# Another order of tasks for ScalarE, SyncE and TensorE in a one-core Mamba and routed-expert kernel

## The chip, the core and the metric

The kernel runs on one core of a Trainium2 chip. The core has TensorE (matrix products, PE in the profile), VectorE (DVE), ScalarE (ACT), GpSimd (POOL) and SyncE (SP, which issues nearly all DMAs). Each engine runs its own instructions strictly in order and waits on semaphores that the others raise. The metric is the device time of one execution in microseconds (us); lower is better. The kernel before takes 2237.96 us, the median of three runs (2236.62 to 2238.84).

## The reference, cut to what matters

```python
x = x + tanh(g_xattn) * mamba(ctx, z=layernorm(x))      # x: [4, 1024, 1024], ctx: [4, 1024, 512]
x = x + tanh(g_ffn)   * experts(layernorm(x))

def mamba(h, z):                                        # 1024 channels, 16 states each
    u  = silu(causal_conv4(in_proj_w @ h) + conv_b)
    dt_low, B, C = split(x_proj_w @ u)                  # 32, 16 and 16 rows
    dt = softplus(dt_proj_w @ dt_low + dt_proj_b)
    state[t] = state[t-1] * exp(dt[t] * A) + dt[t] * u[t] * B[t]
    y[t] = sum over the 16 states of state[t] * C[t] + D * u[t]
    return y * silu(z)

def experts(x):                                         # 16 experts that share one 1024x1024 weight
    S = softmax(x @ router_w + router_b)
    G, idx = top 256 of the 4096 tokens for each expert
    return scatter_add(G * (x[idx] @ expert_w + expert_b))
```

Since all experts share one weight, the product x @ expert_w is computed once for every token, and what each token receives is that row, with the bias, times the sum of its chosen scores. All of it is in float32.

## The kernel before

**Tiling.** The 4 x 1024 tokens are cut into eight halves of 512 tokens (h = 0 to 7), and the 1024 channels into eight blocks of 128 (e = 0 to 7). For each half there are 8 x 16 = 128 rows of states, and each row is one scan over 512 tokens on VectorE (`scan_of`, L1002). A half has 64 *slots*, and a slot is two scans. All five engines run a loop over the slots of a half, and in each slot they do the tasks whose place in a table is that slot; a number below 0 or over 63 means the half before or after. Everything but the scans is software-pipelined by these tables: while half h is scanned, the front of half h + 1 (input projection, convolution, `silu_u`, `xproj`, `low`) and the back of half h − 1 (norm, router logits, expert product) are done in between.

**What a scan needs.** A decay exp(dt·A), computed by ScalarE into one of three PSUM banks (`decays`, L794, one for each scan, so that ScalarE can be at most three scans ahead of VectorE), and an input dt·u·B in one of eight state buffers, made by VectorE (`times_b`, L989) for five groups of eight and by GpSimd (L1236) for the other three. After the scan GpSimd multiplies by C (`times_c`, L1248), and TensorE turns the product and adds it up in the bank pY (`sum_states`, L586), which frees the state buffers. At the end of a channel block VectorE multiplies pY by the gate (`y_out`, L1010) and adds it to x (`add_x`, L1018).

**ScalarE's other tasks.** Some are short copies out of PSUM: `gate_out` (L806, turned gate, after TensorE's `turn_gate`, L597), `xfT_out` (L847), `logits_out` (L876), `unit_out` (L861, a finished 128x512 piece of the expert product), `low` (L760, after TensorE's `xproj`, L563), `xin_ready` (L746, after `inproj`, L554). Three kinds are what is called a burst below: `softplus` (L767, eight times in a half), `silu_u` (L754, once in a half, 4096 columns) and `gate_silu` (L868, twice in a half, 4 x 512 columns). A burst needs another function table, so a table load stands before it and another one (L936) behind it. In a slot the order on ScalarE is: decays, diagonal, `xin_ready`, `low`, `dtu_copy`, the bursts, and then `late`, which holds `gate_out`, `xfT_out`, `logits_out`, `norm_x2`, the row sums and `unit_out`.

**TensorE** does in a slot first `inproj`, `xproj` and `dtproj` (L572, the input of `softplus`), and then `late`: `sum_states`, `turn_gate`, `logits`, `turn_xf` (L612), and `product_step` (L647). A unit of the product (128 tokens x 512 columns) is eight steps, each with its own 128x512 piece of expert_w that SyncE loads into a ring of NRING places (`load_step`, L395). The bank pA is shared by `inproj`, `xproj` and `turn_gate`, the bank pD by `dtproj`, `turn_xf` and `logits`. `turn_xf` waits until the logits before it have been copied out by ScalarE. For the last half (h = 7) the expert weight is resident in the memory that B's rows held, and the ring isn't used.

**SyncE** also walks the slots, and blocks at each DMA that must wait. A load of dt_proj's weights (`load_dtp`, L353) waits for the `dtproj` two blocks before it; a load into the ring waits for the step that last read the place; `load_gate` (L362) waits for the last `turn_gate` that read its tile.

**The end.** After the scans of half 7 come the rest of the product of half 6 and 7, the softmax, a search for each expert's threshold in 30 steps, and a stage in which all rows come back from memory, are scaled, added and written out.

Of the kernel before, what the change touches and what calls it, by code (L numbers as in the profile page):

```python
# [13 lines left out]
P = 128  # L14
# [31 lines left out]
IN_SLOT = [-77, -73] + [GQ * j - 85 for j in range(2, E)]  # L46
# [3 lines left out]
HALO_SLOT, SILU_SLOT = [-24], [-20]  # L50
XP_SLOT, LOW_SLOT = [-18, -18, -17, -17], [-14]
# [14 lines left out]
SZT_SLOT = [GQ * e + 9 for e in range(5)] + [43, 50, 65]  # L66
# [6 lines left out]
XF_SLOT = [s + 4 for s in LN2_SLOT]  # L73
# [7 lines left out]

UNIT_SLOT = [104 + 8 * i for i in range(2 * TT)]
STEP_SLOT = [s + min(k, E - 2) for s in UNIT_SLOT for k in range(E)]
UO_SLOT = [s + 8 for s in UNIT_SLOT]

SLOTTED = 2
NRING, NPIECE = 4, 3
# [4 lines left out]
def at(slots, g, h):  # L92

    return [(i, h - s // G) for i, s in enumerate(slots) if s % G == g and 0 <= h - s // G < NC]
# [29 lines left out]
def mamba_moe(nc, x, ctxT, g_xattn, g_ffn, winT, conv_w, conv_b, xpT, dtpT, dt_b, a_log, dvec,  # L124
              router_w, router_b, expert_w, expert_b, consts, row_masks, out):
    with ExitStack() as ctx:
        def sb(name, shape, dt=F32):
            return ctx.enter_context(nc.sbuf_tensor(name, shape, dt))
# [30 lines left out]
        mhalf = sb("mhalf", [P, B, E])  # L159
# [22 lines left out]
        mv1 = szT[0][:, 160:160 + 2 * NC * TT].rearrange("p (b e s) -> p b e s", b=B, e=E)  # L182
        coef = szT[1][:, 0:TT * NC].rearrange("p (t c) -> p t c", t=TT)
# [149 lines left out]
        def _(sp):  # L333
# [94 lines left out]
            WK_SLOT = [s - 2 for s in STEP_SLOT]  # L428
# [3 lines left out]
            DTW_SLOT = [DTP_SLOT[e] - 17 for e in range(E)]  # L432
# [65 lines left out]
            load_dtp(0, 3)  # L498
# [240 lines left out]
        def _(act):  # L739
# [174 lines left out]
            def half(h):  # L914
                for g in range(G):
# [8 lines left out]
                    for e, k in at(DCP_SLOT, g, h):  # L924
                        dtu_copy(k, e)
                    steps_due = at(SP_SLOT, g, h)
# [10 lines left out]
                    late(h, g)  # L937
# [33 lines left out]
        def _(dve):  # L971
# [138 lines left out]
            nc.vector.memset(mhalf[:], -0.5).then_inc(s_c, 1)  # L1110
# [111 lines left out]
        def _(pool):  # L1222
# [40 lines left out]
            def rstd2(h, t):  # L1263
                wait(pool, s_bn, n(h, 3 * TT, 3 * t + 3))
                nc.gpsimd.tensor_tensor(rs2[:, t:t + 1], ve2[:, t:t + 1], mhalf[:, 0, 0:1], ALU.pow).then_inc(s_pr, 1)
                pool.wait_ge(s_pr, n(h, TT, t + 1))
                nc.gpsimd.tensor_tensor(nb2[:, t:t + 1], nm2[:, t:t + 1], rs2[:, t:t + 1], ALU.mult).then_inc(s_rs2, 1)
# [22 lines left out]
            def ln1_rstd(rows, k):  # L1290
                pool.wait_ge(s_ln1v, k)
                nc.gpsimd.tensor_tensor(ln1[:, rows, 0, :], ve1[:, rows, :], mhalf[:, rows, :], ALU.pow).then_inc(s_rs1, 1)
# [63 lines left out]
```

## Time and profile before

| what | value |
|---|---|
| median of three runs | 2237.96 us |
| the profiled execution, its time and its span | 2250.82 us, 2249.0 us |
| DVE busy | 1936.2 us (86%) |
| POOL busy | 1711.8 us (76%) |
| PE busy | 1668.7 us (74%) |
| ACT busy | 1371.7 us (61%) |
| DVE busy between 980 and 1220 us | 218.31 of 240 us |
| POOL busy between 980 and 1220 us | 213.52 of 240 us |
| mean granted TensorE clock | 0.880 |
| last scan ends | at about 1972.7 us |

How to read it: the busy shares are averages over the whole span, and the stages differ. From about 66 to 1973 us the scans run, about 240 us to a half; from there to about 2090 us VectorE mostly waits, and then the search and the last stage follow. A row of the timeline gives the start, the length, engine, line, operation, tiles, shapes and count, and in brackets how long the engine was idle before it and what ended that idle time. "SPq" is SyncE's queue.

### The profile page before, as it was taken

The page shows a single profiled execution, that of the slowest core. Times are in us where ns is not written, and L with a number is a line of the kernel's source. Part 1 is how long each engine was busy: PE and PEld are TensorE (multiplying, and loading weights), DVE is VectorE, ACT ScalarE, POOL GpSimd, SP SyncE. Part 2 cuts the span into 40 slices and gives each one's busy share as a digit, 9 for nine tenths or more (in the row PEclk, how much of TensorE's full clock was granted, in tenths as well). Part 3 has the DMA queues.
Part 4 walks back from the last instruction along what each step waited for, and adds up shares of the span by engine and source line. Part 5 has one row for each costly group of instructions (what it writes and reads, how often), then busy time and mean ns, then how long its engine had stood idle before and what let it go on. Part 6 is the DMA issues. An engine that isn't in the chain of part 4 may idle for free.

```text
span 2249.0 us, 23467 instructions
## 1 busy us (share of the span) xinstructions
PE 1668.7 (74%) x7564; PEld 1064.5 (47%) x7564; DVE 1936.2 (86%) x2081; ACT 1371.7 (61%) x2326; POOL 1711.8 (76%) x606
## 2 busy tenths in 40 slices
PE   7467676678887888778887888787878787788720
PEld 2235445445554555445554555454555565544310
DVE  7989999988999899988997999889997899910587
ACT  3545766675778676766787676757786767622000
POOL 0578999987899899988998899878998999920000
PEclk9677788889898999999998999899998899999865
DMA  9500141134735383527443563337343734376078
GB/s 370 220 15 29 63 174 66 38 108 147 265 111 169 99 301 113 179 67 279 139 160 96 192 226 119 126 126 270 118 150 100 277 109 136 99 239 231 0 300 353
DMA packets 144219, 358.69 MB, mean 159 GB/s; under 512 B 15586, under 2 KB 18146, under 8 KB 134882
## 3 DMA queue, kind: packets, MB, share of 16 engines
q1 hardware_dynamic: 140354, 343.57, 43.1%
q10 hardware_dynamic: 3744, 13.63, 1.5%
q8 instruction: 61, 1.00, 0.2%
q14 instruction: 60, 0.49, 0.1%
HBM read 310.48 MB, written 46.66 MB: 159 GB/s over the span
## 4 chain that ended last, share of the span: by engine, by line
DVE 25%; PE 23%; issue 16%; POOL 13%; ACT 11%; DMA 9%; SPq 1%; ACTq 1%; DVEq 0%; POOLq 0%
DVE states L1002 15%; POOL states L1248 8%; PE pM L647 7%; PE pY L586 5%; PE pA L554 4%; POOL states L1236 4%; DMA sz<-in_x 4%; DMA wk<-in_expert_w 3%; DVE states L989 3%; ACT pDec L794 3%; DVE u L979 2%; PE pA L563 2%; ACT L936 2%; ACT sz L868 2%; DMA bbc<-x_scratch 1%
## 5 line engine op out<-in xcount | busy, mean ns | idle before, releaser
L1248 POOL TENSOR_TENSOR states<-states,cbc 128x2048 f32<-128x2048 f32 x256 | 1158.3, 4532 | 114.2 <-ACT carry L778 83.0
L794 ACT ACTIVATE pDec<-steps,an 128x512 f32<-128x512 f32 x1024 | 691.7, 687 | 441.9 <-DVE states L1002 439.6
L586 PE MATMUL pY<-con,states 128*128 128x128 f32 x4096 | 578.6, 303 | 144.3 <-POOL states L1248 144.1
L1002 DVE TENSOR_TENSOR_SCAN states<-pDec,carry,states 128x512 f32<-128x512 f32 x512 | 625.2, 1265 | 57.2 <-ACT pDec L794 57.0
L586 PEld LDWEIGHTS pY<-con,states 128*128 128x128 f32 x4096 | 532.9, 158 | 272.0 <-POOL states L1248 220.6
L1002 DVE TENSOR_TENSOR_SCAN states<-pDec,states 128x512 f32<-128x512 f32 x512 | 594.7, 1205 | 66.2 <-ACT pDec L794 65.7
L647 PE MATMUL pM<-wk,xfT 128*128 128x512 f32 x896 | 473.0, 634 | 78.7 <-DMA wk<-in_expert_w 75.4
L1236 POOL TENSOR_TENSOR states<-dtu,bbc 128x1024 f32<-128x1024 f32 x192 | 454.2, 2366 | 98.9 <-PE pY L586 81.4
L989 DVE TENSOR_TENSOR states<-pU,bbc 128x1024 f32<-128x1024 f32 x320 | 385.3, 1204 | 17.3 <-PE pY L586 14.0
L554 PE MATMUL pA<-ctx_sb,win 128*128 128x512 f32 x448 | 233.8, 671 | 53.3 <-issue 32.5
L647 PEld LDWEIGHTS pM<-wk,xfT 128*128 128x128 f32 x896 | 154.3, 202 | 173.3 <-issue 96.3
L554 PEld LDWEIGHTS pA<-ctx_sb,win 128*128 128x128 f32 x448 | 94.2, 217 | 180.5 <-issue 148.1
L582 PE MATMUL pY<-ddiag,u 128*128 128x128 f32 x512 | 84.5, 317 | 106.1 <-issue 88.7
L582 PEld LDWEIGHTS pY<-ddiag,u 128*128 128x128 f32 x512 | 77.5, 225 | 148.9 <-issue 129.2
L979 DVE SCALAR_TENSOR_TENSOR u<-pA,cw,u 128x509 f32<-128x509 f32 x171 | 125.1, 732 | 2.1
L936 ACT ACT_TABLE_LOAD x86 | 110.3, 1283 | 1.5
L1227 POOL TENSOR_TENSOR dtu<-steps,u 128x512 f32<-128x512 f32 x64 | 81.4, 1272 | 11.8 <-ACT steps L767 11.8
L1062 DVE TENSOR_REDUCE mx<-lg 128x4 f32<-128x64 f32 x8 | 1.7, 208 | 96.2 <-ACT lg L876 96.2
L767 ACT ACT_TABLE_LOAD x64 | 82.1, 1283 | 1.1
L572 PE MATMUL pD<-xpr,dtp 32*128 32x512 f32 x128 | 75.5, 670 | 5.1 <-ACT xfT L847 3.3
L861 ACT COPY stg<-pM 128x512 f32<-128x512 f32 x56 | 32.4, 579 | 73.2 <-PE pM L647 73.2
L612 PE MATMUL pD<-con,xr 128*128 128x128 f32 x240 | 39.9, 293 | 38.0 <-ACT lg L876 38.0
(174 smaller groups left out, 1394.9 us busy)
## 6 DMA issues: line engine op xcount, KB each, us to landing
wk<-in_expert_w SPq DMA_DIRECT2D x448, 256.0 KB, 4.2
bbc<-bc_scratch SPq DMA_DIRECT2D x32, 1024.0 KB, 6.5
cbc<-bc_scratch SPq DMA_DIRECT2D x32, 1024.0 KB, 9.0
sz<-in_x SPq DMA_DIRECT2D x16, 1024.0 KB, 7.4
xt<-in_x SPq DMA_DIRECT2D x15, 1024.0 KB, 5.6
win<-in_winT SPq DMA_DIRECT2D x58, 256.0 KB, 2.7
x_scratch<-xt SPq DMA_DIRECT2D x14, 1024.0 KB, 6.9
xr<-x_scratch SPq DMA_DIRECT2D x28, 512.0 KB, 4.2
```

The costliest lines, as they stand in the source:

```text
L554: mm = pe.matmul(pA[:], win[j % 2][:, part, :], ctx_sb[:, part, :], start=(part == 0), stop=(part == KC - 1))
L582: mm = pe.matmul(pY[:, eT(t)], u[h % 2][:, e, eT(t)], ddiag[:], start=(t == 0), stop=False)
L586: mm = pe.matmul(pY[:, eT(t)], states[g % NST][:, i, eT(t)], ident, start=False, stop=(q == QG - 1 and i == QN - 1 and t == TT - 1), is_tr ...
L647: pe.matmul(bank[:], piece_of(h, 2 * t + k // 4)[:, k % 4, :], weights, start=(k == 0), stop=(k == E - 1)) \
L767: nc.scalar.activation(dt[e % 2], pD[:], ACT.Softplus, bias=dtb[:, e:e + 1]).then_inc(s_sp, 1)
L794: nc.scalar.activation(pDec[bank_of(h, k)][:], dt[e % 2], ACT.Exp, scale=an[:, k:k + 1]).then_inc(s_dec, 1)
L936: nc.scalar.preload_act_table_set(EXP)
L979: nc.vector.scalar_tensor_tensor(out=dst, in0=bank[:, 0:T - HALO + i], scalar=cw[:, j, i:i + 1], in1=dst, op0=ALU.mult, op1=ALU.add).then_ ...
L989: nc.vector.tensor_tensor(states[g % NST], spread(pU), bbc[:, QN * q:QN * (q + 1), :], ALU.mult) \
L1002: nc.vector.tensor_tensor_scan(st, pDec[bank_of(h, k)][:], st, 0.0 if h % HB == 0 else carry[:, e, k % NS:k % NS + 1], ALU.mult, ALU.add). ...
L1236: nc.gpsimd.tensor_tensor(states[g % NST], spread(dtu[e % 2]), bbc[:, QN * q:QN * (q + 1), :], ALU.mult) \
L1248: nc.gpsimd.tensor_tensor(st, st, cbc[:, QW * q:QW * (q + 1), :], ALU.mult).then_inc(s_hc, 1)
```

## The change

Only the places of tasks change, with the ring of expert weights and the room for it; no arithmetic does.

```diff
-IN_SLOT = [-77, -73] + [GQ * j - 85 for j in range(2, E)]
+IN_SLOT = [-79, -74] + [GQ * j - 85 for j in range(2, E)]
-HALO_SLOT, SILU_SLOT = [-24], [-20]
-XP_SLOT, LOW_SLOT = [-18, -18, -17, -17], [-14]
+HALO_SLOT, SILU_SLOT = [-24], [-22]
+XP_SLOT, LOW_SLOT = [-20, -20, -19, -19], [-16]
-SZT_SLOT = [GQ * e + 9 for e in range(5)] + [43, 50, 65]
+SZT_SLOT = [GQ * e + 9 for e in range(5)] + [43, 48, 65]
-XF_SLOT = [s + 4 for s in LN2_SLOT]
+XF_SLOT = [s + 5 for s in LN2_SLOT]
-STEP_SLOT = [s + min(k, E - 2) for s in UNIT_SLOT for k in range(E)]
-UO_SLOT = [s + 8 for s in UNIT_SLOT]
+STEP_SLOT = [s + k for s in UNIT_SLOT for k in (0, 1, 1, 2, 3, 3, 4, 5)]
+UO_SLOT = [s + 7 for s in UNIT_SLOT]
-NRING, NPIECE = 4, 3
+NRING, NPIECE = 5, 3
...
-            WK_SLOT = [s - 2 for s in STEP_SLOT]
+            WK_SLOT = [s - 3 for s in STEP_SLOT]
-            DTW_SLOT = [DTP_SLOT[e] - 17 for e in range(E)]
+            DTW_SLOT = [DTP_SLOT[e] - 15 for e in range(E)]
...
             load_dtp(0, 2)
-            load_dtp(0, 3)
...
                     for e, k in at(DCP_SLOT, g, h):
                         dtu_copy(k, e)
+                    late(h, g)
                     steps_due = at(SP_SLOT, g, h)
...
                     if steps_due or silus or gates:
                         nc.scalar.preload_act_table_set(EXP)
-                    late(h, g)
```

Modulo 64, the places near the end of a half are now: `silu_u` in slot 42 (44 before), the four parts of `xproj` in 44 and 45 (46 and 47), `low` in 48 (50), the seventh gate turned in 48 (50) and copied in 49 (51), the first two input projections of the half after next in 49 and 54 (51 and 55). A unit's steps stand in six slots (seven before, of which the last held two), and its copy in the seventh slot after its first step (the eighth before). The fifth place of the ring takes 2 KB of each partition; for it the constant −0.5 shrinks to one column, and the copy that the first norm needs moves into a tile that is free then (one more short memset).

**ScalarE, where `silu_u` stands** (middle of the scans of half 4; `u1` is the front of half 5, `szT0` a gate's copy, `lg` the logits). Before:

```order
L794 ACTIVATE pDec0<-steps,an 128x512
L778 COPY carry<-states1 128x2
L794 ACTIVATE pDec1<-steps,an 128x512
L754 ACT_TABLE_LOAD
L754 ACTIVATE u1<-u1 128x4096
L936 ACT_TABLE_LOAD
L806 COPY szT0<-pA 128x512
L876 COPY lg<-pD 128x16
L794 ACTIVATE pDec2<-steps,an 128x512
```

With the change:

```order
L795 ACTIVATE pDec0<-steps,an 128x512
L807 COPY szT1<-pA 128x512
L755 ACT_TABLE_LOAD
L755 ACTIVATE u1<-u1 128x4096
L938 ACT_TABLE_LOAD
L795 ACTIVATE pDec1<-steps,an 128x512
L779 COPY carry<-states0 128x2
L795 ACTIVATE pDec2<-steps,an 128x512
L795 ACTIVATE pDec0<-steps,an 128x512
L779 COPY carry<-states1 128x2
L795 ACTIVATE pDec1<-steps,an 128x512
L807 COPY szT0<-pA 128x512
```

The burst stands four decays earlier, the short copy `szT1` of its slot in front of it, and the copies `szT0` and `lg`, which stood right behind it, now come four decays after it.

**ScalarE, from the product's copy to the next burst** (the same half, slots 47 to 50; `stg` is `unit_out`, `xpr` is `low`). Before:

```order
L861 COPY stg<-pM 128x512
L794 ACTIVATE pDec1<-steps,an 128x512
L778 COPY carry<-states3 128x2
L794 ACTIVATE pDec2<-steps,an 128x512
L798 ACTIVATE ddiag<-con,dvt 128x128
L767 ACT_TABLE_LOAD
L767 ACTIVATE steps<-pD,dtb 128x512
L936 ACT_TABLE_LOAD
L794 ACTIVATE pDec0<-steps,an 128x512
L778 COPY carry<-states0 128x2
L794 ACTIVATE pDec1<-steps,an 128x512
L760 ACTIVATE xpr<-pA,csc 64x512
```

With the change:

```order
L862 COPY stg<-pM 128x512
L795 ACTIVATE pDec2<-steps,an 128x512
L779 COPY carry<-states3 128x2
L795 ACTIVATE pDec0<-steps,an 128x512
L761 ACTIVATE xpr<-pA,csc 64x512
L795 ACTIVATE pDec1<-steps,an 128x512
L779 COPY carry<-states3 128x2
L795 ACTIVATE pDec2<-steps,an 128x512
L799 ACTIVATE ddiag<-con,dvt 128x128
L807 COPY szT1<-pA 128x512
L768 ACT_TABLE_LOAD
L768 ACTIVATE steps<-pD,dtb 128x512
```

Between the product's copy and the burst there are four decays in place of two, and both `xpr` and the seventh gate's copy `szT1` (which came later than this piece before) stand in front of the burst.

**TensorE, where the second input projection stands** (the same half, slots 52 to 56; `win1` is its weight, `dtp0` that of `dtproj`). Before:

```order
L582 MATMUL pY<-ddiag,u0 128x128 x4
L586 MATMUL pY<-con,states0 128x128 x16
L647 MATMUL pM<-wk,xfT 128x512 x2
L586 MATMUL pY<-con,states1 128x128 x16
L647 MATMUL pM<-wk,xfT 128x512 x2
L554 MATMUL pA<-ctx_sb,win1 128x512 x4
L572 MATMUL pD<-xpr,dtp0 128x512
L586 MATMUL pY<-con,states2 128x128 x16
```

With the change:

```order
L583 MATMUL pY<-ddiag,u0 128x128 x4
L587 MATMUL pY<-con,states0 128x128 x16
L648 MATMUL pM<-wk,xfT 128x512 x2
L555 MATMUL pA<-ctx_sb,win1 128x512 x4
L587 MATMUL pY<-con,states1 128x128 x16
L573 MATMUL pD<-xpr,dtp0 128x512
L587 MATMUL pY<-con,states2 128x128 x16
```

The projection stands one group of sums earlier, and no longer right in front of `dtproj`. The convolution of the block before it, for which it waits, also stands two slots earlier on VectorE (52 and 53 in place of 54 and 55).

## Rows read from the trace of the kernel before

**Rows 1.** Who waited for whom, whole span: total us, times, longest us

```profile
DVE states L1002 <- ACT pDec L794: 122.7, 71, 4.9
...
ACT stg L861 <- PE pM L647: 73.2, 20, 6.6
...
ACT sz L868 <- DMA sz<-in_x: 10.9, 7, 3.1
```

**Rows 2.** SyncE's own waits, whole span

```profile
SPq L353 <- PE pD L572: 739.8, 60, 31.1
```

**Rows 3.** Timeline of ScalarE in half 4, slots 44 to 58

```profile
1197.56 1.28 ACT L754 ACT_TABLE_LOAD   x1
1198.85 3.62 ACT L754 ACTIVATE u<-u 128x4096 f32<-128x4096 f32 x1
...
1204.33 0.71 ACT L794 ACTIVATE pDec<-steps,an 128x512 f32<-128x512 f32 x1
...
1219.92 0.58 ACT L861 COPY stg<-pM 128x512 f32<-128x512 f32 x1 [6.64 <-PE pM L647]
...
1234.40 0.59 ACT L806 COPY szT<-pA 128x512 f32<-128x512 f32 x1 [3.29 <-PE pA L597]
...
1258.75 0.69 ACT L767 ACTIVATE steps<-pD,dtb 128x512 f32<-128x512 f32 x1 [4.27 <-PE pD L572]
```

**Rows 4.** Timeline of VectorE, the same stretch

```profile
1197.85 0.67 DVE L1010 TENSOR_TENSOR pY<-pY,szT 128x512 f32<-128x512 f32 x1
1198.43 1.21 DVE L989 TENSOR_TENSOR states<-pU,bbc 128x1024 f32<-128x1024 f32 x1
...
1205.14 4.57 DVE L1002 TENSOR_TENSOR_SCAN states<-pDec,states 128x512 f32<-128x512 f32 x4 [1.53 <-ACT pDec L794]
...
1261.54 2.34 DVE L1002 TENSOR_TENSOR_SCAN states<-pDec,states 128x512 f32<-128x512 f32 x2 [3.82 <-ACT pDec L794]
```

**Rows 5.** Timeline of TensorE, the same stretch

```profile
1204.69 1.08 PE L612 MATMUL pD<-con,xr 128*128 128x128 f32 x4 [5.88 <-ACT lg L876]
...
1210.81 1.88 PE L647 MATMUL pM<-wk,xfT 128*128 128x512 f32 x4
1212.62 3.65 PE L563 MATMUL pA<-u,xp 128*64 128x512 f32 x8
1216.20 1.97 PE L586 MATMUL pY<-con,states 128*128 128x128 f32 x16
...
1251.10 6.56 PE L554 MATMUL pA<-ctx_sb,win 128*128 128x512 f32 x8 [3.24 <-issue]
```

**Rows 6.** VectorE's waits between 482.2 and 524.0 us (half 1, slots 44 to 52)

```profile
DVE states L1002 <- ACT pDec L794: 8.4, 5, 2.6
DVE states L989 <- PE pY L586: 1.9, 2, 1.3
DVE pY L1010 <- PE pY L586: 1.2, 1, 1.2
```

**Rows 7.** VectorE's waits between 1683.2 and 1723.2 us (half 6, the same slots)

```profile
DVE states L1002 <- ACT pDec L794: 8.3, 5, 2.7
DVE states L989 <- PE pY L586: 2.6, 2, 1.5
```

**Rows 8.** VectorE's waits between 538.0 and 547.8 us (half 1, slot 58)

```profile
DVE states L1002 <- ACT pDec L794: 3.4, 1, 3.4
```

**Rows 9.** VectorE's waits between 1497.0 and 1506.9 us (half 5, slot 58)

```profile
DVE states L1002 <- ACT pDec L794: 3.5, 1, 3.5
```

**Rows 10.** Who waited for whom between 1975 and 2042 us

```profile
PE pM L647 <- DMA wk<-in_expert_w: 9.9, 6, 3.8
```

**Rows 11.** Timeline of ScalarE, copies of finished units behind the last scan

```profile
1991.59 0.58 ACT L861 COPY stg<-pM 128x512 f32<-128x512 f32 x1 [2.15 <-PE pM L647]
...
2039.47 0.58 ACT L861 COPY stg<-pM 128x512 f32<-128x512 f32 x1 [6.37 <-PE pM L647]
...
2077.07 0.58 ACT L861 COPY wk<-pM 128x512 f32<-128x512 f32 x1 [2.29 <-PE pM L647]
```

More of the change, by code:

```diff
@@ L158, in mamba_moe @@
         ddiag = sb("ddiag", [P, P])
-        mhalf = sb("mhalf", [P, B, E])
+        mhalf = sb("mhalf", [P, 1])
         ctx_sb = sb("ctx_sb", [P, KC, T])
@@ L182, in mamba_moe @@
         mv1 = szT[0][:, 160:160 + 2 * NC * TT].rearrange("p (b e s) -> p b e s", b=B, e=E)
+        mhalves = szT[0][:, 280:280 + NC * TT].rearrange("p (b e) -> p b e", b=B)
         coef = szT[1][:, 0:TT * NC].rearrange("p (t c) -> p t c", t=TT)
@@ L1109, in _ @@
             nc.vector.memset(one[:], 1.0)
-            nc.vector.memset(mhalf[:], -0.5).then_inc(s_c, 1)
+            nc.vector.memset(mhalf[:], -0.5)
+            nc.vector.memset(mhalves, -0.5).then_inc(s_c, 1)
             dve.wait_ge(s_w, 16 * NW)
@@ L1264, in rstd2 @@
                 wait(pool, s_bn, n(h, 3 * TT, 3 * t + 3))
-                nc.gpsimd.tensor_tensor(rs2[:, t:t + 1], ve2[:, t:t + 1], mhalf[:, 0, 0:1], ALU.pow).then_inc(s_pr, 1)
+                nc.gpsimd.tensor_tensor(rs2[:, t:t + 1], ve2[:, t:t + 1], mhalf[:], ALU.pow).then_inc(s_pr, 1)
                 pool.wait_ge(s_pr, n(h, TT, t + 1))
@@ L1291, in ln1_rstd @@
                 pool.wait_ge(s_ln1v, k)
-                nc.gpsimd.tensor_tensor(ln1[:, rows, 0, :], ve1[:, rows, :], mhalf[:, rows, :], ALU.pow).then_inc(s_rs1, 1)
+                nc.gpsimd.tensor_tensor(ln1[:, rows, 0, :], ve1[:, rows, :], mhalves[:, rows, :], ALU.pow).then_inc(s_rs1, 1)
             ln1_rstd(slice(0, 1), 1)
```

## The prediction

> **What bounds the kernel now.** I read the busy shares first, then who waited for whom, then the timelines of three engines side by side around VectorE's longest waits, and last the stretch behind the last scan. While the scans run, VectorE is busy 218.31 of 240 us, so about 20 us of each half are not VectorE's own work (table of the profile, 980 to 1220 us). The list of waits says what those are: 122.7 us in 71 waits of a scan for its decay [rows 1]. ScalarE is busy 61% of the span, so it isn't short of time: it is late at a few places, because it is held by a burst or by somebody else's result. These places are the same in each half:
>
> - Slots 44 to 52. In half 4 `silu_u` with its two table loads holds ScalarE from 1197.56 to 1203.8 [rows 3]; the first scan behind it waits 1.53 us [rows 4]. The logits' copy stands behind the burst, and TensorE waits 5.88 us for it [rows 5]. From there TensorE works without a gap for 15.2 us, up to the unit's end, for which ScalarE's copy waits 6.64 us with no decay ready behind it; and the seventh gate's copy waits 3.29 us more [rows 3]. VectorE loses 11.5 us here in half 1 (8.4 + 1.9 + 1.2) [rows 6] and 10.9 us in half 6 [rows 7]; the six halves 1 to 6 lie between 8.8 and 12.0 (half 4) and make 63.6 us, 10.6 each. Half 0, which has no product beside it, loses 1.7.
> - Slot 58. TensorE waits 3.24 us for a convolution, makes the second input projection in 6.56 us [rows 5] and only then `dtproj`; `softplus` waits 4.27 us for it [rows 3] and VectorE 3.82 [rows 4]. It is 3.4 us in half 1 [rows 8] and 3.5 in half 5 [rows 9], 15.3 in the five halves 1 to 5, and 1.3 in half 0. Half 6, which has no such projection to make (there is no half 8), has no wait there: that is the control for the cause.
> - Slots 6 and 38, behind `gate_silu`. The one in slot 6 is longer, since the gate's tile lands late: ScalarE waits 10.9 us for it in 7 cases [rows 1].
>
> Behind the last scan TensorE is the bound. The units of half 6, whose weights come through the ring, end 12.0 us apart (2039.47 − 1991.59 over 4); the next four, with resident weights, 9.4 us (2077.07 − 2039.47 over 4) [rows 11]. 9.9 us are plain waits for the ring [rows 10].
>
> **The change, part by part.**
>
> *`silu_u` two slots up.* The burst is 1.28 + 3.62 + 1.28 = 6.2 us, then comes a decay of 0.7. Before, VectorE had beside it the gate's product (0.67 [rows 4]), the add behind it (as long), two inputs (1.21 each) and two scans (1.14 each from the 4.57 of four), 6.0 us in all, and 1.5 were left open. In slot 42 the product and the add (they belong to slots 43 and 44) and one input fall behind the burst: 2.3 us of scans, one input of 1.2 and some 0.3 of a scan already running are the cover, 3.8 us, and the chain is 0.6 (the gate copy now in front) + 6.2 + 0.8 = 7.6. The hole grows from 1.5 to about 3.8, so 2.3 to 2.4 us are lost in each of seven halves. The halo sums on GpSimd for `silu_u` end some 2 us behind its new start in the odd halves' fronts, while the table loads; that costs nothing to 1 us, and I take nothing.
>
> The trace shows 6.2 us for this burst, from the table load at 1197.56 to the copy after the second load, so a load costs 1.28 and nothing more. The Trainium skill (ScalarE: Activation LUTs, What ACT_TABLE_LOAD costs) puts about 1.38 us of drain on top of each load, 2.66 for every switch. By that the moved burst would be longer by 2.7 us, uncovered in its new place, and seven halves would put 19 us on the sum. The row decides against it here, and the sum below goes by the row.
>
> *`xproj`, `low`, the unit's copy and the gate's copy.* What is bought with it: four decays stand between burst and logits' copy, but the burst is two slots (7.5 us) up, so TensorE resumes about 2 us earlier than 1204.69. Up to the unit's end its work is as long as before: one sum group of 2.0 us and a step of 0.94 fewer, the second `xproj` of 3.65 more [rows 5], 15.9 against 15.2 us. So the unit ends about 1.4 us earlier, but ScalarE asks for it one slot earlier: VectorE's hole there (4.1 us, its wait for TensorE's sums included) stays near 4. The next burst now has four decays in front of it instead of two, with the gate's copy waiting some 1 us: 1.0 + 0.6 + 3.25 + 0.7 = 5.5 against a lead of 3.8, a hole of 1.7. The hole that the late gate copy makes in slots 51 and 52 goes. New sum: 3.8 + 4 + 1.7 = 9.5 for 10.6 before, a gain of 1.1 in six halves, and 2.4 lost in half 0: +6.6 − 2.4 = 4 us gained. The bounds are wide, since three in-order engines meet here: if only the burst's own hole is left, (10.6 − 3.8) x 6 − 2.4 = 38 gained; if nothing of the rest goes, 7 x 2.4 = 17 lost. I stay near the hand-worked value.
>
> *Input projections at 49 and 54.* The convolution that the second one waits for is done two slots earlier and it stands before a sum group, no longer between the steps and `dtproj`. The 4.27 us of ScalarE go, and the hole with it; late there is then the burst itself, which leaves VectorE no hole at the other places where nothing holds it. 15.3 + 1.3, less about 0.5 in each of six: 13 us gained. Bounds 0 and 16.6.
>
> *SyncE's order and the ring.* Today SyncE stands 739.8 us at `load_dtp` [rows 2], because this load stands one slot ahead of the product it waits for; the weights of the next unit and the B and C rows are queued behind it and then go out in a heap, in front of the gate's tile. Two slots later the wait is met when SyncE gets there. The B and C rows leave earlier and the gate's tile has fewer in front of it. Against that, the loads of the sixth and seventh step now wait for the unit's first two steps, so the gate's load goes out one step (0.94 us) later. I take 3 us gained of the 10.9; bounds 10.9 gained and 7 x 0.94 = 7 lost. Waits for weights during the scans cost VectorE nothing by themselves, as far as ScalarE's copy of the unit isn't reached.
>
> *The tail.* A load goes out when the step four (now five) before is done, and four steps of 0.94 don't cover the time to its landing, as the 9.9 us of waits show; five are one step nearer to it. The most there is to win is 5 units x (12.0 − 9.4) = 13 us. The stretch begins with 4 MB of resident weights in front of the ring's loads, and no ring hides that; four steps instead of two are loaded ahead of it. I take 8; bounds 0 and 13.
>
> Part of the tail's loss is TensorE's clock: in the stretch behind each wait a step takes up to twice as long as later in the unit, as the second projection does (6.56 us against 3.65 for the equally long `xproj` [rows 5]). It is contained in the 12.0.
>
> *At nothing:* `norm_x2` a slot later (it waits less for GpSimd, and TensorE asks for it four slots later); the seventh gate's turn; one memset more at the start, beside loads; the `dtproj` weights no longer loaded ahead, since 32 rows have a slot and more to land.
>
> *Sum.* 4 + 13 + 3 + 8 = 28 us. From the profiled 2250.82 that makes 2223; this execution is 12.9 us over the median of the runs, and against the median 2237.96 it makes 2210.
>
> **Rivals.**
>
> 1. *The cluster opens up.* If TensorE, no longer held by the logits, is early enough that neither the unit's copy nor the gate's waits, the burst's hole alone is left: 34 us more than my sum, at most; half of that is 2193. For it: 6.64 and 3.29 us of waiting are more than what the place itself costs. Against: `xproj` is in front of the unit's last step now.
> 2. *The ring and the projections give less than they should* (the tail's transfers land as late as before, and slot 58 is closed only by half): −8 − 6, 2224. For it: the 4 MB burst. Against: the steps whose weights are there run without any wait.
> 3. *Slower.* The burst eats VectorE's cover and everything behind it shifts: seven holes of 2.4 more (17 us), and the gate's copy, now in front of the `softplus` burst with no decay between them, adds its whole wait to the burst. Before, the same copy waited 3.29 us apart from any burst. If it waits as long, 3.3 − 1.0 = 2.3 more in six halves is 14, and the unit's copy, asked for a slot earlier with TensorE no earlier, 3.7 in six halves 22. On top of my sum, which holds the seven holes already: 2210 + 14 + 22 = 2246. It decides from 4.7 us more in each of six halves on, since 28 us is all that my sum has to lose. For it: a wait in front of a burst is the worst place for one. Against: TensorE resumes 2 us earlier, and has no stall for weights.
> 4. *It does nothing*: the holes only move, since VectorE and GpSimd (213.52 of 240 us in the same table) share the states' buffers: 2234 to 2242.
>
> **Chances.** My forecast 0.48, rival 1 0.16, rival 2 0.17, rival 3 0.10, rival 4 0.09. The range of 8 in 10 reaches from 2193 (rival 1 at half) to 2238 (rival 4); my own case alone is 2202 to 2218. A difference under 0.2% (4.5 us) can't be told from none here: faster by more 0.81, within it 0.08, slower by more 0.11.
>
> **What would show it.** Right: the hole behind `silu_u` at 3.5 to 4 us in each half, and TensorE's wait for the logits near 4 in place of 5.88; `dtproj` done before `softplus` asks in slot 57, and no hole of VectorE in slot 58; SyncE's 739.8 us at `load_dtp` mostly gone, moved to the ring's waits; the ring's units behind the last scan 10 to 10.5 us apart; VectorE's 122.7 us at 95 to 100. Wrong: the copy of the unit waiting over 8 us, or the gate's copy over 3 us right in front of `softplus`; units in the tail still 12 us apart.

## The result, and the profile after

| | before | changed |
|---|---|---|
| median, eight runs each | 2237.29 us (2234.88 to 2243.97) | 2230.37 us (2228.37 to 2235.79) |
| ratio of changed to before | | 0.997, 95% interval 0.9957 to 0.9984 |
| span of the profiled execution | 2249.0 us | 2234.0 us |
| end of the last scan | 1972.7 us | 1971.1 us |
| from there to the softmax of half 7 | 114.0 us | 100.2 us |
| DVE, PE busy | 1936.2, 1668.7 us | 1934.1, 1677.9 us |
| mean granted TensorE clock | 0.88 | 0.86 |

The change makes the kernel 6.9 us faster where 28 were forecast. The two profiled executions differ by more than the medians, 15.0 us, because that of before lay 13 us over its median and that of the changed kernel 5 us. What follows compares executions place by place; of those 15.0 us only 1.6 are there when the last scan ends, and 13.4 come behind it (13.8 up to the softmax, with 0.4 lost again after it).

The lists of waits answer to [rows 1] and [rows 2], first the engines, then SyncE's own queue (total us, times, longest us):

```profile
DVE states L1003 <- ACT pDec L795: 131.3, 51, 6.5
...
ACT stg L862 <- PE pM L648: 65.3, 16, 7.5
...
PE pD L613 <- ACT lg L877: 39.4, 9, 8.4
...
ACT sz L869 <- DMA sz<-in_x: 9.7, 5, 4.7
```

```profile
SPq L397 <- PE pM L648: 706.8, 281, 11.7
...
SPq L355 <- PE pD L573: 265.2, 60, 34.1
```

VectorE waits for decays in 20 places fewer (51 for 71), but 8.6 us longer in all; the prediction had named 95 to 100 us as the sign of being right. SyncE's wait has moved from `load_dtp` to the ring, as forecast. To see why the remaining waits are long, the three engines are read side by side in half 4 again, slots 41 to 49. ScalarE, against [rows 3]:

```profile
1191.39 1.28 ACT L938 ACT_TABLE_LOAD   x1
1192.69 0.69 ACT L795 ACTIVATE pDec<-steps,an 128x512 f32<-128x512 f32 x1
...
1194.02 0.57 ACT L807 COPY szT<-pA 128x512 f32<-128x512 f32 x1
1194.62 1.28 ACT L755 ACT_TABLE_LOAD   x1
1195.91 3.62 ACT L755 ACTIVATE u<-u 128x4096 f32<-128x4096 f32 x1
...
1203.99 0.17 ACT L877 COPY lg<-pD 128x16 f32<-128x16 f32 x1
...
1221.24 0.58 ACT L862 COPY stg<-pM 128x512 f32<-128x512 f32 x1 [7.43 <-PE pM L648]
```

VectorE, against [rows 4]:

```profile
1193.83 2.33 DVE L1003 TENSOR_TENSOR_SCAN states<-pDec,states 128x512 f32<-128x512 f32 x2
1201.63 2.34 DVE L1003 TENSOR_TENSOR_SCAN states<-pDec,states 128x512 f32<-128x512 f32 x2 [5.47 <-ACT pDec L795]
...
1222.52 2.34 DVE L1003 TENSOR_TENSOR_SCAN states<-pDec,states 128x512 f32<-128x512 f32 x2 [4.11 <-ACT pDec L795]
...
1231.07 2.34 DVE L1003 TENSOR_TENSOR_SCAN states<-pDec,states 128x512 f32<-128x512 f32 x2 [1.73 <-ACT pDec L795]
```

TensorE, against [rows 5]:

```profile
1204.41 1.08 PE L613 MATMUL pD<-con,xr 128*128 128x128 f32 x4 [4.13 <-ACT lg L877]
...
1208.84 4.03 PE L564 MATMUL pA<-u,xp 128*64 128x512 f32 x8
...
1216.50 3.65 PE L564 MATMUL pA<-u,xp 128*64 128x512 f32 x8
...
1246.10 3.67 PE L555 MATMUL pA<-ctx_sb,win 128*128 128x512 f32 x8 [0.31 <-issue]
```

Three things are to be seen. The table load behind the `softplus` of slot 41 ends at 1192.67, and 1.95 us later the burst of slot 42 begins; only two decays fit between, so VectorE has one pair of scans (1193.83 to 1196.16) for a burst of 6.2 us and stands 5.47 us. The logits' copy still stands behind the burst, and TensorE waits 4.13 us for it. That looks like the gain that was forecast (near 4 for 5.88), but only halves 2, 4 and 6 are like this: in halves 1, 3 and 5 the same wait is 7.5 to 8.4 us, and over the six halves it is 36.2 us where it was 36.6 before. Both `xproj` parts then come before the unit's last step, and its copy waits 7.43 us. The projection at 1246.10, on the other hand, takes 3.67 us in place of 6.56, and behind half 0 no `softplus` waits for `dtproj` any more: VectorE has no wait at all in slot 58 of any half.

VectorE's waits in half 6, slots 43 to 52 (1676 to 1722 us), answer to [rows 7]; those of half 1, which answer to [rows 6], came to 10.6 + 0.4 us:

```profile
DVE states L1003 <- ACT pDec L795: 11.6, 4, 5.5
DVE states L990 <- PE pY L587: 0.8, 1, 0.8
```

Halves 0 and 7 have a new hole, that of the gate's copy in front of `softplus` (timeline of ScalarE, two places, and VectorE behind the first):

```profile
280.13 0.59 ACT L807 COPY szT<-pA 128x512 f32<-128x512 f32 x1 [2.87 <-PE pA L598]
...
1922.92 0.59 ACT L807 COPY szT<-pA 128x512 f32<-128x512 f32 x1 [4.04 <-PE pA L598]
```

```profile
284.82 4.57 DVE L1003 TENSOR_TENSOR_SCAN states<-pDec,states 128x512 f32<-128x512 f32 x4 [5.04 <-ACT pDec L795]
```

The wait of 4.04 us in half 7 is over the 3 us that the prediction had named as a sign of being wrong.

Behind the last scan, copies of finished units as in [rows 11], and TensorE's wait for the ring as in [rows 10]:

```profile
1985.05 0.58 ACT L862 COPY stg<-pM 128x512 f32<-128x512 f32 x1 [2.69 <-PE pM L648]
...
2024.85 0.58 ACT L862 COPY stg<-pM 128x512 f32<-128x512 f32 x1 [2.26 <-PE pM L648]
...
2062.45 0.58 ACT L862 COPY wk<-pM 128x512 f32<-128x512 f32 x1 [1.44 <-PE pM L648]
```

```profile
PE pM L648 <- DMA wk<-in_expert_w: 1.4, 2, 0.9
```

The ring's units end 9.95 us apart (39.80 over 4) for 12.0, and 1.4 us of ring waits are left of 9.9.

VectorE's idle times, added up by slot over both traces, give the account (us):

| place | before | changed | gained | forecast |
|---|---|---|---|---|
| slots 43 to 52, halves 1 to 6 | 63.6 | 70.4 | −6.8 | +6.6 |
| the same, half 0 | 1.7 | 10.5 | −8.8 | −2.4 |
| the same, half 7 | 0 | 4.0 | −4.0 | 0 |
| slot 58 | 16.6 | 0 | +16.6 | +13 |
| slot 55 | 2.1 | 0 | +2.1 | 0 |
| slot 6, halves 1 to 7 | 23.8 | 22.4 | +1.4 | +3 |
| last scan to the softmax | 114.0 | 100.2 | +13.8 | +8 |

Each kernel was profiled a second time (below, with the fifth experiment). There the gains of the first five rows come out within 1 us or, in the first row, 2 us of these, but slot 6 gives 9.3 us (30.6 to 21.3) and the tail 10.7 (109.7 to 99.0). These two rows therefore vary between executions; the others hold in both pairs.

### The profile page after: what moved, and what is told of

Its sections match the earlier page's. It is cut to its first block, busy times and chain, and to the rows that moved or that the text cites. A ratio compares the mean times of both kernels' runs of the same rounds, so it can differ in the third digit from the quotient of the medians.

```text
span 2234.0 us, 23468 instructions
## 1 busy us (share of the span) xinstructions
PE 1677.9 (75%) x7564; PEld 1090.5 (49%) x7564; DVE 1934.1 (87%) x2082; ACT 1372.6 (61%) x2326; POOL 1711.5 (77%) x606
## 4 chain that ended last, share of the span: by engine, by line
DVE 26%; POOL 19%; PE 18%; issue 16%; ACT 14%; DMA 5%; ACTq 1%; SPq 0%; DVEq 0%; POOLq 0%
DVE states L1003 16%; POOL states L1250 11%; POOL states L1238 6%; PE pM L648 6%; PE pY L587 5%; ACT pDec L795 4%; DVE states L990 3%; PE pA L555 2%; DVE u L980 2%; DMA sz<-in_x 2%; ACT L938 2%; PE pA L564 2%; ACT L768 1%; ACT sz L869 1%; POOL dtu L1229 1%
## 5 line engine op out<-in xcount | busy, mean ns | idle before, releaser
L587 PE MATMUL pY<-con,states 128*128 128x128 f32 x4096 | 601.5, 310 | 185.4 <-POOL states L1250 185.4
L587 PEld LDWEIGHTS pY<-con,states 128*128 128x128 f32 x4096 | 555.3, 162 | 306.2 <-POOL states L1250 254.4
L648 PE MATMUL pM<-wk,xfT 128*128 128x512 f32 x896 | 464.8, 634 | 6.3 <-DMA wk<-in_expert_w 3.3
L555 PE MATMUL pA<-ctx_sb,win 128*128 128x512 f32 x448 | 227.1, 654 | 44.7 <-issue 19.6
L648 PEld LDWEIGHTS pM<-wk,xfT 128*128 128x128 f32 x896 | 162.2, 207 | 112.0 <-issue 94.3
L583 PEld LDWEIGHTS pY<-ddiag,u 128*128 128x128 f32 x512 | 72.4, 214 | 140.1 <-issue 122.0
L862 ACT COPY stg<-pM 128x512 f32<-128x512 f32 x56 | 32.4, 578 | 65.3 <-PE pM L648 65.3
```

What stands on the lines that cost most here:

```text
L555: mm = pe.matmul(pA[:], win[j % 2][:, part, :], ctx_sb[:, part, :], start=(part == 0), stop=(part == KC - 1))
L583: mm = pe.matmul(pY[:, eT(t)], u[h % 2][:, e, eT(t)], ddiag[:], start=(t == 0), stop=False)
L587: mm = pe.matmul(pY[:, eT(t)], states[g % NST][:, i, eT(t)], ident, start=False, stop=(q == QG - 1 and i == QN - 1 and t == TT - 1), is_tr ...
L648: pe.matmul(bank[:], piece_of(h, 2 * t + k // 4)[:, k % 4, :], weights, start=(k == 0), stop=(k == E - 1)) \
```

## The experiments

Unless something else is said, each is the changed kernel with one edit. Ratios are to the kernel before, run in the same batch. The first four share one chip and its runs of before (median 2245.85 us), the next four another (2248.53), the last three a third (2246.49). "Idle" and "tail" are the columns of the account above: VectorE's idle time in the scans, and the time from the last scan to the softmax.

**`softplus` one slot earlier.** The hole behind `silu_u` was put down to the `softplus` just in front of it.

```diff
-DTP_SLOT = [GQ * e - 9 for e in range(E)]
-SP_SLOT = [GQ * e - 7 for e in range(E)]
+DTP_SLOT = [GQ * e - 9 - (e == 6) for e in range(E)]
+SP_SLOT = [GQ * e - 7 - (e == 6) for e in range(E)]
```

> The changed kernel with the seventh dtproj and its softplus one slot earlier (38 and 40 in place of 39 and 41), so that one slot of decays stands between this burst and silu_u in slot 42. My theory: the hole behind silu_u is 5.1 to 5.5 us and not the 3.8 that I worked out, because ScalarE comes straight from the softplus of slot 41 and has no lead. Then the hole in slot 43 falls to about 3.8 in seven halves, 1.5 us each: about 10 us less than the changed kernel, 2220. Rival: the hole is the silu burst's own (TensorE, GpSimd or the halo sums set it): slot 43 stays at 5.1 to 5.5 and the time at 2230.

Measured: 2232.99 us, ratio 0.9951 (0.9935 to 0.9968), not to be told from the changed kernel's 0.993 (0.9912 to 0.9948) below. In halves 1, 3 and 5 the hole fell from 5.08 to 3.6, as expected. In halves 2, 4 and 6 it grew from 5.47 to 7.05, and in half 0 to 6.48. ScalarE and GpSimd in half 4 say why:

```profile
1189.66 0.58 ACT L807 COPY szT<-pA 128x512 f32<-128x512 f32 x1
1193.50 1.28 ACT L755 ACT_TABLE_LOAD   x1 [3.27 <-POOL u L1263]
```

```profile
1187.44 4.53 POOL L1250 TENSOR_TENSOR states<-states,cbc 128x2048 f32<-128x2048 f32 x1 [2.72 <-ACT carry L779]
...
1192.48 0.95 POOL L1263 TENSOR_TENSOR u<-u,halw 128x24 f32<-128x24 f32 x3
```

Asked for 3 us earlier, `silu_u` waits for GpSimd's halo sums, which stand behind a product of 4.53 us. So in halves 1, 3 and 5 the neighbour was the cause of what lay over the forecast: with it moved away the hole is 3.6, near the forecast 3.8. In the other halves this run can't show it, since a second in-order engine, GpSimd, bounds how early the burst can stand at all.

**`late` behind the bursts again.**

```diff
-                    late(h, g)
                     steps_due = at(SP_SLOT, g, h)
...
                         nc.scalar.preload_act_table_set(EXP)
+                    late(h, g)
```

> The changed kernel with ScalarE's short tasks behind the bursts again (that one edit undone). My theory: the gate's copy in front of softplus in slot 49 holds the burst for TensorE's turn, which costs VectorE 5.0 us in half 0 and 4.0 in half 7; behind the burst both fall below 1.5, and the hole behind silu_u shrinks by the 0.6 us of the copy that stood in front of it, 4 us in seven halves: about 10 us less, 2220. Rival: the short tasks in front feed TensorE earlier, and without that the input projection in slot 49 waits for the copy: holes in slots 50 to 52 grow by 1 us or more in six halves, 2235 to 2240.

Measured: 2239.06 us, ratio 0.9972 (0.9953 to 0.9991). The holes of slot 50 in halves 0 and 7 fell from 5.0 and 4.0 to 2.1 and 0.5. New ones came in slot 51 of halves 0 to 5 (1.6 to 3.5), where VectorE's product of pY now waits for TensorE's sums (half 4):

```profile
1245.47 0.70 DVE L1011 TENSOR_TENSOR pY<-pY,szT 128x512 f32<-128x512 f32 x1 [3.29 <-PE pY L587]
```

The hole of slot 43 stayed (5.05 to 5.45), so the gate's copy in front of the burst has no part in it. The theory's 10 us of gain didn't come: the median is 7 us over the 2232.2 of the changed kernel, though on another chip, and VectorE's idle time in the scans is 154.8 us for its 145.7 and 143.6. So the front place seems to be worth a few us even with `silu_u` in slot 42.

**Input projections back.**

```diff
-IN_SLOT = [-79, -74] + [GQ * j - 85 for j in range(2, E)]
+IN_SLOT = [-77, -73] + [GQ * j - 85 for j in range(2, E)]
```

> The changed kernel with the first two input projections back in slots 51 and 55. My theory: the hole in slot 58, gone with the change (16.6 us of VectorE's idle time), comes back in halves 1 to 5: 10 to 15 us more than the changed kernel, 2240 to 2245. Rival: that hole went because TensorE is no longer held by the ring's loads or by the old places of the steps; then it stays away and the time is 2228 to 2233.

Measured: 2252.39 us, ratio 1.0032 (1.0016 to 1.0048). The holes of slot 58 are back (14.1 us in all), and the rest is as in the changed kernel but for slot 6 (26.3 us for 22.4). The forecast's term of 13 us is confirmed by the holes; the time itself is 20 us over that of the changed kernel on another chip, more than the 10 to 15 expected. Without this part the change would have been no faster than before.

**A ring of four, loaded two slots ahead.**

```diff
-NRING, NPIECE = 5, 3
+NRING, NPIECE = 4, 3
...
-            WK_SLOT = [s - 3 for s in STEP_SLOT]
+            WK_SLOT = [s - 2 for s in STEP_SLOT]
```

> The changed kernel with four places in the ring and its loads two slots ahead again. My theory: the 13.9 us between the two profiles behind the last scan (114.0 us before and 100.1 after, from the last scan to the softmax of half 7) come from the fifth place: the units of half 6 end 12 us apart again, 10 to 14 us more than the changed kernel, 2241 to 2244, nearly all of it behind the last scan. Rival: the new places of the steps or SyncE's freed queue brought it: the tail stays within 3 us of 100, and the time within 4 us of 2230.

Measured: 2231.43 us, ratio 0.9939 (0.9918 to 0.9961), the same time as with five. The tail is 107.0 us for 99 to 100, as expected, but the scans end 9.4 us earlier than in the second profile of the changed kernel (1959.2 for 1968.6). All seven holes of slot 6 are 1.8 to 2.0 us. The theory had 10 to 14 us more than the changed kernel; what it had not seen is this gain in slot 6, which cancels the longer tail. So the ring is two edits, its places and its lead, and they have to be tried apart.

**The changed kernel, and the one before, once more**, in the batch of the next two.

> The changed kernel itself, on the chip of the runs beside it, as their reference. Every theory expects 0.997 of before again (within 0.995 and 0.999), last scan at 1969 to 1973 us, softmax of half 7 100 us behind it, holes of 5.1 to 5.5 us in slot 43, about 4 in slot 48, 5.0 and 4.0 in slot 50 of halves 0 and 7.

> The kernel before, once more with a profile, since its first profiled execution lies 13 us over its median. If that is chance, this one comes in nearer its median, with the same holes; if the profile itself costs time, it is again about 2250. Every theory expects the tail from the last scan to the softmax of half 7 at 112 to 116 us.

Measured: 2232.22 us, ratio 0.993 (0.9912 to 0.9948); and 2248.22 us for one execution of before. The ratio is below the 0.995 to 0.999 that was expected, because before is slower on this chip. The second profile of before has a tail of 109.7 us, outside the 112 to 116 expected, and that of the changed kernel 99.0. The changed kernel's median is nearly the same on the two chips where it ran (2230.4 and 2232.2); that of before is 2237.3 on one chip and 2246 to 2249 on three. Before's idle time in slot 6, where it waits for a transfer, was 23.8 us in one profile and 30.6 in the other. So the change is worth 7 to 16 us, by where before is run.

**Five places, loaded two slots ahead.**

```diff
-            WK_SLOT = [s - 3 for s in STEP_SLOT]
+            WK_SLOT = [s - 2 for s in STEP_SLOT]
```

> The changed kernel with five places in the ring but its loads two slots ahead, as before. My theory: with loads three slots ahead SyncE stands at the ring's place in slots 0 and 1, in front of the gate's load of slot 2, and that alone makes the holes in slot 6 (up to 6.5 us) and about 12 us of the scans' time; two slots ahead slot 6 falls to 1.8 to 2.0 in all halves as with four places, the last scan ends near 1960, and the tail stays at 100 us: about 10 us less than the changed kernel. Rival: the fifth place itself does it, by more weights in flight beside the B and C rows; then slot 6 keeps holes over 2.5 us and the scans end near 1971.

Measured: 2222.36 us, ratio 0.9885 (0.9867 to 0.9903), 9.9 us less than the changed kernel in the same batch, as expected. The tail is 99.4 us, and the seven holes of slot 6 are 1.8 to 2.0 again, 13.3 us in all for 21.3. Half 7, slot 6, in the changed kernel, on SyncE's queue, ScalarE and VectorE:

```profile
1751.12 8.86 SPq L397 DMA_DIRECT2D wk<-in_expert_w  x2
...
1762.05 0.45 SPq L364 DMA_DIRECT2D sz<-in_x  x1
```

```profile
1774.73 2.93 ACT L869 ACTIVATE sz<-sz,ln 128x512 f32<-128x512 f32 x4 [4.70 <-DMA sz<-in_x]
```

```profile
1779.77 2.46 DVE L1003 TENSOR_TENSOR_SCAN states<-pDec,carry,states 128x512 f32<-128x512 f32 x2 [6.51 <-ACT pDec L795]
```

And in this experiment:

```profile
1753.68 0.42 SPq L364 DMA_DIRECT2D sz<-in_x  x1
```

```profile
1763.21 2.93 ACT L869 ACTIVATE sz<-sz,ln 128x512 f32<-128x512 f32 x4
```

```profile
1768.25 2.46 DVE L1003 TENSOR_TENSOR_SCAN states<-pDec,carry,states 128x512 f32<-128x512 f32 x2 [1.82 <-ACT pDec L795]
```

In the changed kernel the gate's load left at 1762.05 and was waited for until 1774.73, 12.7 us later; in the experiment `gate_silu` started 9.5 us after the load left, without a wait. SyncE stood 8.86 us at the ring in front of it, with the loads of three slots ahead. How much of the delay is its later start and how much a slower transfer beside more of the ring's, these runs don't separate.

**The half's end back where it was**: `silu_u`, `xproj`, `low` and the seventh gate two slots down, the projections too, with `late` still in front of the bursts.

```diff
-IN_SLOT = [-79, -74] + [GQ * j - 85 for j in range(2, E)]
-HALO_SLOT, SILU_SLOT = [-24], [-22]
-XP_SLOT, LOW_SLOT = [-20, -20, -19, -19], [-16]
-SZT_SLOT = [GQ * e + 9 for e in range(5)] + [43, 48, 65]
+IN_SLOT = [-77, -73] + [GQ * j - 85 for j in range(2, E)]
+HALO_SLOT, SILU_SLOT = [-24], [-20]
+XP_SLOT, LOW_SLOT = [-18, -18, -17, -17], [-14]
+SZT_SLOT = [GQ * e + 9 for e in range(5)] + [43, 50, 65]
```

> The changed kernel with the half's end back: silu_u in slot 44, xproj 46 and 47, low 48 to 50, the seventh gate turned in 50 and copied in 51, and the first two projections in 51 and 55 (they can't stand in 49 with these). Against the kernel that has only the projections back (1.0032 of before). My theory: the half's end two slots up costs 5 us of hole behind silu_u for 1.5, about 10 us in all over seven halves, and 9 us in slots 49 and 50 of halves 0 and 7; all comes back, and since ScalarE's short tasks now stand in front of silu_u in its own slot 44, the logits' copy is out before the burst and TensorE's wait of 4 to 6 us goes: 20 to 30 us less than with only the projections back, 0.990 to 0.994 of before. Rival: the two slots are needed for xproj and low, and holes of 2.5 us in slots 49 to 52 return: within 5 us of 1.0032.

Measured: 2189.94 us, ratio 0.9737 (0.9716 to 0.9759). ScalarE, VectorE and TensorE in half 4:

```profile
1177.12 0.58 ACT L807 COPY szT<-pA 128x512 f32<-128x512 f32 x1 [1.90 <-PE pA L598]
1177.60 0.18 ACT L877 COPY lg<-pD 128x16 f32<-128x16 f32 x1
1177.79 1.28 ACT L755 ACT_TABLE_LOAD   x1
...
1189.02 0.58 ACT L862 COPY stg<-pM 128x512 f32<-128x512 f32 x1
```

```profile
1184.82 4.57 DVE L1003 TENSOR_TENSOR_SCAN states<-pDec,states 128x512 f32<-128x512 f32 x4 [3.54 <-ACT pDec L795]
...
1202.18 2.34 DVE L1003 TENSOR_TENSOR_SCAN states<-pDec,states 128x512 f32<-128x512 f32 x2 [0.49 <-ACT pDec L795]
```

```profile
1178.03 0.63 PE L613 MATMUL pD<-con,xr 128*128 128x128 f32 x4 [0.95 <-ACT lg L877]
```

In slot 44 the logits are ready when the burst is due, and with `late` in front their copy gets through first. TensorE waits 0.95 us for it, not 5.88 [rows 5] or 4.13, and the unit is done before ScalarE asks. Of the holes of slots 43 to 52 only that of the burst is left, 1.4 to 3.5 us, with one of 0.5 in slot 51 of every second half; those of slot 58 are back (16.5 us). Against the experiment with the projections back, from which this one differs by the half's end alone, VectorE's idle time falls from 160 to 102 us, and the time by 62 (by the medians of two batches, 2252.39 and 2189.94). The theory had 20 to 30. The four tasks of the half's end were moved together, so what each of them is worth isn't shown by this run.

**`late` in front, and nothing else**, in the kernel before (its edit there is the reverse of that of the second experiment).

> The kernel before with one edit of the change alone: ScalarE's short tasks in front of the bursts. My theory after the run with the half's end back: the cluster of slots 45 to 52 hangs on the logits' copy of slot 44 standing behind silu_u; in front of it TensorE resumes some 6 us earlier, the unit's copy and the gate's copy don't wait, and of 10.6 us in each of six halves 1.5 to 3 are left: 45 to 55 us less than before, 0.976 to 0.980. Rival: the gain came from the steps in six slots and the ring with it (the unit is done a slot earlier); then this edit alone gives under 20 us, over 0.991.

Measured: 2213.03 us, ratio 0.985 (0.9823 to 0.9876), so 33 us less than before from moving one line. TensorE's wait for the logits is 0.95 again, and the hole behind the burst 3.02:

```profile
1183.51 0.63 PE L612 MATMUL pD<-con,xr 128*128 128x128 f32 x4 [0.95 <-ACT lg L876]
...
1206.69 1.10 PE L647 MATMUL pM<-wk,xfT 128*128 128x512 f32 x2 [1.50 <-DMA wk<-in_expert_w]
```

```profile
1190.31 4.57 DVE L1002 TENSOR_TENSOR_SCAN states<-pDec,states 128x512 f32<-128x512 f32 x4 [3.02 <-ACT pDec L794]
```

It is less than the 45 to 55 expected, and more than the rival's 20; the holes of slot 50 (0.4 to 2.7 us) stayed. TensorE still waits 79.6 us for its expert weights (75.4 before), and `softplus` 24.0 us for `dtproj` (28.9 before). The size of the ring isn't the reason: with a ring of four in the changed kernel TensorE's wait for these weights is 6.3 us. What is left from before here is SyncE's stand at `load_dtp`, 738.8 us, and the old places of the steps; which of the two matters wasn't tried.

**The logits one slot earlier**, so that their copy gets in front of the burst in slot 42 too.

```diff
-LG_SLOT = [106 + 16 * t for t in range(TT)]
-LGA_SLOT = [s + 2 for s in LG_SLOT]
+LG_SLOT = [105 + 16 * t for t in range(TT)]
+LGA_SLOT = [s + 1 for s in LG_SLOT]
```

> The changed kernel with silu_u left in slot 42, but the logits made in slot 41 and copied in slot 42, and so in front of the burst (every logits task one slot, every copy two slots earlier). My theory: what the change loses is the logits' copy behind the burst; with it in front, TensorE's wait of 4.1 us before turn_xf is under 1, the unit's copy of slot 47 waits little, and the holes of 4.1 us in slot 48 of six halves fall under 1; those of 5.1 to 5.5 in slot 43 stay or grow by what the copy waits for the logits: 10 to 20 us less than the changed kernel, 2212 to 2222. Rival: it is silu_u's place two slots up that costs (TensorE has both xproj parts in front of the unit's last step); then slot 48 keeps over 3 us and the time stays within 5 of 2232.

Measured: 2236.05 us, ratio 0.9959 (0.9941 to 0.9976), no gain. ScalarE, VectorE and TensorE in half 4:

```profile
1189.09 0.17 ACT L877 COPY lg<-pD 128x16 f32<-128x16 f32 x1 [0.87 <-PE pD L629]
1189.28 1.28 ACT L755 ACT_TABLE_LOAD   x1
...
1212.53 0.59 ACT L862 COPY stg<-pM 128x512 f32<-128x512 f32 x1 [4.04 <-PE pM L648]
```

```profile
1196.30 2.34 DVE L1003 TENSOR_TENSOR_SCAN states<-pDec,states 128x512 f32<-128x512 f32 x2 [6.52 <-ACT pDec L795]
...
1213.81 2.34 DVE L1003 TENSOR_TENSOR_SCAN states<-pDec,states 128x512 f32<-128x512 f32 x2 [1.66 <-ACT pDec L795]
```

```profile
1198.82 5.34 PE L564 MATMUL pA<-u,xp 128*64 128x512 f32 x8 [2.75 <-ACT szT L807]
```

The expected 10 to 20 us of gain did not come. The mechanism is confirmed in its place: the holes of slot 48 fall from 24.3 to 5.0 us. But the copy now waits 0.87 us in front of the burst, whose hole grows to 5.2 to 6.8, and the next short copy, that of the gate in slot 44, still stands behind the burst and holds `xproj` for 2.75 us. Slots 11, 27 and 59, each one slot behind a new place of the logits' copy, lose 20.3 us in place of 5.9 in the changed kernel. The scans end 5.7 us earlier than in the second profile of the changed kernel, and the tail is 9.7 longer. Why the tail grew wasn't found.

**Put together**: the half's end back, `late` in front, five places loaded two slots ahead, and the second and third input projection one slot later than in the kernel before, so that the second stands behind the `dtproj` of slot 55 and not in front of it.

```diff
-IN_SLOT = [-79, -74] + [GQ * j - 85 for j in range(2, E)]
+IN_SLOT = [-77, -72, -68] + [GQ * j - 85 for j in range(3, E)]
...
-            WK_SLOT = [s - 3 for s in STEP_SLOT]
+            WK_SLOT = [s - 2 for s in STEP_SLOT]
```

(with the other three lines of the half's end as above)

> The kernel of the half's end back (0.9737) with the ring's loads two slots ahead and the second and third projections in slots 56 and 60, behind dtproj and not in front of it. If the causes add: slot 6 falls to 1.8 to 2.0 (as with five places two ahead, 9.9 us less there) and the holes of 2.5 to 3.6 us in slot 58 of five halves close (14 to 16 us): 0.962 to 0.966 of before, 2163 to 2173. Rival: the third projection, closer to the softplus of slot 65, opens a hole there instead, 2180 to 2190.

Measured: 2161.86 us, ratio 0.9627 (0.9605 to 0.965), 84.6 us under the kernel before on that chip. In the list of waits VectorE's wait for decays is half of [rows 1]:

```profile
DVE states L1003 <- ACT pDec L795: 63.8, 43, 3.9
```

The idle time in the scans is 73.5 us for 146, slot 58 has none, and no hole of slot 6 is over 2.6. The time is what the two causes added up to (0.962 to 0.966 expected).

## Why the prediction was wrong

The sign was right, and the time lies in its range. The size was not: 28 us forecast, 6.9 measured. The sign was owed in part to luck: the half's end lost 19.6 us where 4 were to be gained, and it was slot 58 and the tail that gave more than I had put on them. By the steps of the prediction:

- **The step that failed: "*`silu_u` two slots up*" and the sum "3.8 + 4 + 1.7 = 9.5 for 10.6 before" behind it.** Forecast +4 us for all halves, measured −19.6. The terms of 4 and 1.7 came out in halves 1 to 6 (4.1 and 1.7). The 3.8 was 5.1 to 5.5, and short by 1.5 in seven halves: I counted the scans that lie beside the burst but not that the `softplus` of slot 41 had just used up ScalarE's lead. In half 4 the chain was as long as forecast (7.6 us, from the gate's copy at 1194.02 to the scan at 1201.63), but VectorE's cover was 2.1 us of it, up to 1196.16, and not 3.8. The first experiment shows the cause in halves 1, 3 and 5: with that `softplus` a slot away the hole is 3.6. In the others GpSimd's halo sums take its place as the bound. That the halo "costs nothing to 1 us" was right only as long as the burst was as late as this.
- A comparison of 9.5 with 10.6 also left out the small holes of slots 46 and 51 (4.7 us in six halves), where VectorE waits for TensorE's sums or a decay. With 1.5 in seven halves and the gate's copy (next point) they make up the miss: 10.5 + 4.7 + 9.0 = 24.2, for 23.6.
- **The gate's copy in front of `softplus`** was priced by half 4 and set to about 1 us for all halves. It cost nothing of its own there, but 5.0 and 4.0 us of VectorE in halves 0 and 7. Rival 3's mechanism was real in those two halves and absent in the six that I gave it; putting `late` back takes 5.0 and 4.0 to 2.1 and 0.5, and opens 2.0 in slot 51 of half 0.
- **"TensorE resumes about 2 us earlier"** took the logits' copy to stand behind a burst in any case. The wait didn't fall by it (36.6 to 36.2 us over six halves). More was missed here, though it isn't in the sum: [rows 5] show the 5.88 us, and the same edit that puts `late` in front would have ended them if `silu_u` had stayed in slot 44. The half's end moved back gives 62 us, and `late` in front alone 33. Rival 1 ("the cluster opens up") had the mechanism: with the half's end back, slots 43 to 52 lose 17.5 us in place of 65.3, 47.8 gained where my bound for the opened cluster was 38. I gave as its condition that TensorE be early enough; what it needed was the order of two rows on ScalarE, and `silu_u` in its old slot with it. The order alone, with `silu_u` left in slot 42, closes slot 48 but leaves 42.2 us in slot 43 and 17.3 in slot 50; with the half's end back these are 15.8 in slot 45 and nothing in slot 50.
- **Input projections at 49 and 54**: 13 forecast, 16.6 in slot 58 and 2.1 in slot 55; undone, 14.1 come back. Right.
- **SyncE's order and the ring**: 3 forecast, 1.4 measured in one pair of profiles and 9.3 in the other. The 739.8 us at `load_dtp` went to 265.2, as said. But this was a sum of a gain and a loss: loading three slots ahead alone costs 9.9 us, 8.0 of them in slot 6 behind the gate's tile. I had priced the later gate load at one step (0.94 us), by steps of TensorE, and not by how long SyncE stands in front of it.
- **The tail**: 8 forecast, 13.8 measured, over the upper bound of 13, and 10.7 in the second pair of profiles. Units 9.95 us apart (10 to 10.5 said). Five places against four, in kernels that differ in nothing else but on two chips, are 7.6 us of it (107.0 and 99.4). That a step is slower "behind each wait" was said too widely: in the kernel before, four steps took 5.37 us behind the wait of 2.46 at 2010.33 (mean granted clock 0.66 from 2010 to 2015 us), but 3.60 in an unbroken stretch (1.00 from 1998 to 2003), and the step behind the wait of 0.69 at 2001.94 took 1.13 us.
- **Table loads**: the burst ran 6.2 us again, from 1194.62 to 1200.84, as the row of before had it; the Trainium skill's 1.38 us on top of each load (ScalarE: Activation LUTs, What ACT_TABLE_LOAD costs) is in none of the rows here. The larger hole of slot 43 isn't that: the first experiment brings it to 3.6 in three halves with the same loads.

The gains of the account's table (places of the scans and tail) sum to 14.3 us of the 15.0 between the profiled spans.

What stays open: why half a per cent of before's time varies from chip to chip, which the changed kernel's doesn't on the two chips where it ran (before's waits for the gate's tile vary, and I did not isolate them); what `silu_u`, `xproj`, `low` and the seventh gate are each worth in their places; and the longer tail with the logits a slot earlier.

## What to carry to other kernels

Where an engine in order carries both long bursts and short copies for which another engine waits, write out the order of rows around each burst, and ask of every short copy whether its input is there when the burst starts: in front it costs 0.2 us, behind it 6 on the other engine, and from there on whatever that engine's lateness reaches. When two edits meet at one place, price them apart and together: here `late` in front was worth 33 us by itself, and the half's end moved up cost 62 beside it. A prefetch that goes out earlier on a shared in-order queue is paid for by what stands behind it in that queue, here with 9.9 us.

## What the runs showed of the hardware

- A table load took 1.28 us in every case. In front of a `softplus` that waits for TensorE it ran ahead of the wait: with `late` in front alone, the load is at 1200.92 and its activation waits 1.12 us, until 1203.33. In front of the `silu_u` that waited for GpSimd it stood still with it, until 1193.50, so its 1.28 us came on top. I did not find out what decides this.
- TensorE's mean granted clock was 0.88 before, 0.86 in the changed kernel and 0.874 in the fastest one, whose time is 3.7% shorter than before's. The mean clock doesn't rank these kernels. Single steps differ with the clock granted to them: the same projection took 6.56 us [rows 5] behind a wait of 3.24, at a mean granted clock of 0.56 (most of it at the lower level, 1.2 GHz), and 3.67 at 1246.10 at 1.00 (2.4 GHz).
